# Attention kernel of two layers: statistics of x from four buffers, low weight halves on GpSimd, early first rows, VectorE's row loop unrolled by two

## What is computed

```python
def _gn(v, G=32, eps=1e-5):
    g = v.reshape(B_, H_, W_, G, C_ // G)
    m = jnp.mean(g, axis=(1, 2, 4), keepdims=True)
    s = jnp.var(g, axis=(1, 2, 4), keepdims=True)
    return ((g - m) / jnp.sqrt(s + eps)).reshape(v.shape)

# in_data = _gn(x); q, k, v are projections of it, q scaled by 32 ** -0.5
logits = einsum('abhqc,abhkc->abhqk', q, k) + mask_bias + nonbatched_bias[:, None]
weights = softmax(logits, axis=-1)
wavg = einsum('abhqk,abhkc->abhqc', weights, v)
gate = sigmoid(einsum('abld,ed->able', in_data, Wg) + gating_bias)
x = x + einsum('able,oe->ablo', gate * wavg, Wo) + bo
```

## Time and profile before

| | us |
|---|---|
| median of 3 runs | 3712.91 |
| lowest, highest | 3711.34, 3713.08 |
| the profiled execution: its time | 3713.87 |
| its span (first to last instruction) | 3712.1 |

### The profile page before, as it was taken

The page is one execution under the profiler, slowest core; times in us unless marked ns, Lnnn a source line. Parts: engine busy times, 40 slices in busy tenths (PEclk is TensorE's granted clock), DMA queues, the critical chain, the costliest instruction groups (busy, mean ns, idle before and its releaser), DMA issues.

```text
span 3712.1 us, 122419 instructions
## 1 busy us (share of the span) xinstructions
PE 3487.4 (94%) x36360; PEld 2625.9 (71%) x36360; DVE 3470.5 (93%) x11689; ACT 2890.9 (78%) x5393; POOL 3022.9 (81%) x2056
## 2 busy tenths in 40 slices
PE   0499999999999999999969999999999999999997
PEld 0377777777777777777747777777777777777775
DVE  6599999999999999999959999999999999999997
ACT  0388888888888888888857777778777777777785
POOL 1288888888888888888857888888888888888887
PEclk9999999999999999999989999999999999999999
DMA  8555555555555555555535556566556665566653
GB/s 319 176 117 117 116 115 117 114 119 116 116 115 116 117 117 116 115 118 114 117 112 112 118 117 118 116 121 119 117 117 119 117 121 117 117 118 117 119 119 76
DMA packets 450645, 454.09 MB, mean 122 GB/s; under 512 B 42880, under 2 KB 445440, under 8 KB 445968
## 3 DMA queue, kind: packets, MB, share of 16 engines
q1 hardware_dynamic: 241680, 251.85, 38.3%
q10 hardware_dynamic: 208896, 201.38, 19.6%
HBM read 182.39 MB, written 67.24 MB: 67 GB/s over the span
## 4 chain that ended last, share of the span: by engine, by line
PE 92%; DVE 3%; DMA 3%; issue 1%; POOL 1%; SPq 1%; ACT 1%; DVEq 0%; POOLq 0%; ACTq 0%
PE proj_b L743 19%; PE proj_a L743 18%; PE av_bank L770 13%; PE max_bank L754 13%; PE exp_bank L759 12%; PE proj_a L797 9%; PE den_bank L777 6%; PE proj_b L788 2%; DMA bias_k<-in_xT 1%; DVE stats L589 1%; DMA k_stack<-k_lo 1%; DVE max_bank L656 1%; DVE probs L669 0%; SPq L334 0%; POOL probs_sum L415 0%
## 5 line engine op out<-in xcount | busy, mean ns | idle before, releaser
L656 DVE CUSTOM_DVE_ANT_0 max_bank<-max_bank,bias_q 128x256 f32<-128x256 f32 x4096 | 1643.8, 443 | 156.4 <-PE max_bank L754 132.5
L415 POOL TENSOR_TENSOR probs_sum<-probs 128x1024 f32<-128x1024 f32 x512 | 1208.2, 2360 | 291.2 <-ACT probs L439 152.5
L669 DVE TENSOR_TENSOR probs<-exp_bank,bias_k 128x512 f32<-128x512 f32 x2048 | 1391.7, 680 | 7.4 <-PE exp_bank L759 7.4
L754 PE MATMUL max_bank<-k_stack,q_stack 96*128 96x256 f16 (+1 forms) x4096 | 788.0, 273 | 13.9 <-DMA k_stack<-k_lo 11.9
L759 PE MATMUL exp_bank<-q_stack,k_stack 100*128 100x256 f16 x4096 | 783.2, 272 | 9.6 <-DVE probs L669 6.3
L439 ACT ACTIVATE probs<-probs,mask_bias 128x1024 f32<-128x1024 f32 x512 | 572.8, 1148 | 61.4 <-DVE probs L669 61.2
L656 DVE DVE_READ_ACCUMULATOR2_ANT row_max<- 128x1 f32 x4096 | 573.1, 140 | 0.0
L442 ACT ACTIVATE probs<-probs 128x1024 f32<-128x1024 f32 x512 | 524.7, 1053 | 51.4 <-DVE probs L669 51.4
L770 PE MATMUL av_bank<-probs,v_sb 128*32 128x256 f32 x8192 | 549.3, 386 | 3.1 <-ACT probs L439 1.6
L754 PEld LDWEIGHTS max_bank<-k_stack,q_stack 96*128 96x128 f16 (+1 forms) x4096 | 381.2, 98 | 166.0 <-DVE row_max L656 104.3
L759 PEld LDWEIGHTS exp_bank<-q_stack,k_stack 100*128 100x128 f16 x4096 | 394.2, 97 | 72.6 <-DVE probs L669 11.5
(11 more groups left out here) (132 smaller groups left out, 7049.9 us busy)
## 6 DMA issues: line engine op xcount, KB each, us to landing
q_stack<-q_hi SPq DMA_DIRECT2D x512, 128.0 KB
k_stack<-k_hi SPq DMA_DIRECT2D x512, 128.0 KB
x_in<-in_xT ACTq DMA_DIRECT2D x128, 256.0 KB, 2.7
q_stack<-q_lo SPq DMA_DIRECT2D x256, 128.0 KB
k_stack<-k_lo SPq DMA_DIRECT2D x256, 128.0 KB
y<-in_xT ACTq DMA_DIRECT2D x128, 256.0 KB, 2.9
layer_out<-y ACTq DMA_DIRECT2D x128, 256.0 KB, 2.7
x_in<-layer_out ACTq DMA_DIRECT2D x128, 256.0 KB, 2.7
```

The costliest lines, as they stand in the source:

```text
L415: pool.tensor_tensor(probs_sum[:, g], pr[:, :, 0, :], pr[:, :, 1, :], ALU.add).then_inc(sum_ready, 1)
L656: op = dve.tensor_tensor_reduce(out=max_bank[h % 2][:, t, :], in0=max_bank[h % 2][:, t, :], in1=bias_q[:, h, t, :], scale=1.0 / FINE, scal ...
L669: dve.tensor_tensor(probs[:, r.ring(2), h], exp_bank[h % 2][:, :, :], bias_k[:, h], ALU.add).then_inc(logits_ready, 1)
L754: op = pe.matmul(bank_[:, t, :], q[0:n, t * P:(t + 1) * P], k[0:n, :], start=True, stop=True)
```

## The change

It touches four places. (1) `STAT_TOK` becomes 1024 and there are four buffers of 1 MB, each of the two old ones cut in half: 32 pieces instead of 16. SyncE issues the first four pieces ahead of everything else, then the weights, the mask, the constants, and the rest of the pieces in two loops; the loads of rows 0 and 1 into `x_in` stand between these loops. VectorE's statistics are cut into two loops as well, with the preparation of the mask between them. (2) The low halves of the weights go from VectorE (10 scalar_tensor_tensor) to GpSimd, which needs two instructions for each (a product in place, then a difference). (3) ScalarE loads the table of the square root before it waits for the spread; for layer 1, rows 0 and 1 of x1 are loaded by SyncE in the slot after the last row of layer 0. (4) VectorE's row loop holds two slots instead of four, three kinds of waits are gone or replaced (`shift_psum`, `gate_ready`; `av_psum` and `sum_ready` become `den_psum`), and `gate_tanh` is addressed by a register.

```diff
-STAT_TOK = 2048
+STAT_TOK = 1024
 STAT_LOADS = ROWS * TOK // STAT_TOK
+STAT_BUFS = 4
...
+    def ring_slice(self, n):
+        if isinstance(self.turns, int):
+            return bass.ds(self.off % n, 1)
+        return bass.ds((self.turns * self.unroll + (self.off + n)) % n, 1)
...
-        x_stat = [t.rearrange("p h t k -> p (h t k)").rearrange("p (c t) -> p c t", c=CT)
-                  for t in (probs[:, 1], bias_k[:, :, :, :])]
+        x_stat = [t.rearrange("p h t k -> p (h t k)").rearrange("p (i c t) -> p i c t", i=2, c=CT)[:, i]
+                  for t in (probs[:, 1], bias_k[:, :, :, :]) for i in range(2)]
...
+            def load_stat(c):
+                for i in range(STAT_BUFS):
+                    wait(sp, stat_used, STAT_BUFS * c + (i + 1 - STAT_BUFS), sp_passed)
+                    sp.dma_start(x_stat[i], channel_major(a["xT"], c * (STAT_BUFS * STAT_TOK) + i * STAT_TOK, STAT_TOK)
+                                 ).then_inc(stat_in[i], 16)
...
+                    if l == 0 and s.off == ROWS:
+                        sp.wait_ge(x_norm_ready, ROWS)
+                        for i in range(2):
+                            sp.wait_ge(y_out[i], 16 * (ROWS // 2 - 4))
+                            sp.dma_start(x_in[:, i], channel_major(x1, i * TOK, TOK)).then_inc(x_loaded[i], 16)
...
+            def low_weights(stage, hi, lo):
+                pool.tensor_scalar(stage, stage, W_SCALE, 1.0, ALU.mult, ALU.mult).then_inc(w_scaled, 1)
+                pool.wait_ge(w_scaled, next(scaled))
+                pool.tensor_tensor(lo[:, :, :], stage, hi[:, :, :], ALU.subtract).then_inc(w_lo_ready, 1)
...
                 r = s.plus(2)
-                if r.active():
+                if r.active() and s.active():
...
             for l in range(2):
+                act.preload_act_table_set("sqrt_and_others")
                 act.wait_ge(norm_avg, 2 * l + 2)
...
-                if h == 0:
-                    wait(dve, shift_psum, r.plus(-2).count(1, 1))
                 wait(dve, max_psum, r.count(8, h + 1), dve_passed)
...
-                    wait(dve, av_psum, r.plus(-2).count(2, h // 4 + 1))
-                    wait(dve, sum_ready, r.plus(-2).count(2, h // 4 + 1))
+                    wait(dve, den_psum, r.plus(-2).count(2, h // 4 + 1))
...
                 dve.wait_ge(av_psum, r.count(2, 2))
-                dve.wait_ge(gate_ready, r.count(1, 1))
                 wait(dve, gated_ready, r.plus(-1).count(1, 1))
-                dve.scalar_tensor_tensor(out=avg[:, :, :], in0=gate_tanh[:, r.ring(4)], scalar=1.0,
+                dve.scalar_tensor_tensor(out=avg[:, :, :], in0=gate_tanh[:, r.ring_slice(4)].rearrange(
+                    "p o g t -> p (o g) t"), scalar=1.0,
...
-                slots(dve, l, slot)
+                slots(dve, l, slot, 2)
```

More of the change, by code:

```diff
@@ L30 @@
+import itertools
 import concourse.bass as bass
@@ L271, in _ @@
                 sp.dma_start(out_bias[:, i, :], a[n]).then_inc(const_in, 16)
[L272 to L286, removed]
+            with sp.Fori(1, 3) as c:
+                load_stat(c)
             sp.wait_ge(zeroed, 3)
@@ L289, in _ @@
                 sp.dma_start(stack[1][MASK_ROW:MASK_ROW + 4, i], a["k_rows"]).then_inc(stack_init, 16)
+            for i in range(2):
+                sp.dma_start(x_in[:, i], channel_major(a["xT"], i * TOK, TOK)).then_inc(x_loaded[i], 16)
+            with sp.Fori(3, STAT_LOADS // STAT_BUFS) as c:
+                load_stat(c)
             sp.wait_ge(mask_step, 3)
@@ L358, in _ @@
             pool.wait_ge(zeroed, 3)
+            for l in range(2):
+                for m in range(4):
+                    pool.wait_ge(w_hi_ready, 4 * l + m + 1)
+                    low_weights(w_stage[:, l, m], w_hi[l][m], w_lo[l][m])
+            for l in range(2):
+                pool.wait_ge(w_hi_ready, 8 + l + 1)
+                low_weights(w_out_stage[:, l], w_out_hi[l], w_out_lo[l])
             pool.wait_ge(const_in, 96)
@@ L569, in _, with statistics @@
         def _(dve):
[L571 to L581 removed]
             n = STAT_TOK // 512
[L584 to L585 removed]
+            def statistics(c):
+                for i in range(STAT_BUFS):
                     dve.wait_ge(stat_in[i], c * 16 + 16)
@@ L588, in _ @@
                         for t in range(n):
-                            op = dve.bn_stats(stats[:, ct, bass.ds(c * (2 * n) + (i * n + t), 1), :],
+                            op = dve.bn_stats(stats[:, ct, bass.ds(c * (STAT_BUFS * n) + (i * n + t), 1), :],
                                               x_stat[i][:, ct, t * 512:(t + 1) * 512])
                     op.then_inc(stat_used, 1)
+            with dve.Fori(0, 3) as c:
+                statistics(c)
             dve.wait_ge(mask_in, 32)
@@ L603, in _ @@
             dve.tensor_scalar(mask_pc[:, 1, :], mask_row[:, :], 1.0 / FINE, None, ALU.mult).then_inc(mask_step, 1)
+            with dve.Fori(3, STAT_LOADS // STAT_BUFS) as c:
+                statistics(c)
             def normalisation(l):
```

47 lines of the change are left out of this document (23 added, 24 removed).

## The result

The changed kernel takes a median of 3687.42 us (six executions, 3683.72 to 3689.72) against 3712.83 us for the kernel before (six, 3711.34 to 3713.72). The ratio is 0.9928, with a 95% interval of 0.9917 to 0.9939: faster by 0.7%, 25.4 us. The forecast was 3682.4, in a range of 3673 to 3694.

What follows compares the result with a forecast made beforehand. The prediction took the rows as bound by TensorE, with VectorE close behind, and the start by x's loads and small steps. Savings of 20.8 + 8.1 + 1.6 = 30.5 us gave 3682.4 us, range 3673 to 3694.

Steps and rivals of the forecast that it cites:

- The statistics: Start of the kernel: with four buffers, statistics end at 98 us and aggregation starts 20.8 us sooner, between 17 and 24.
- VectorE can nearly keep up: Statistics: a piece costs VectorE 2.42 us against 2.5 for its data, and the buffers' stock makes up for mask instructions.
- The slow stream: Rival, statistics: a stream that never pauses runs at 361 GB/s, not 421, giving 3693.7 us; chance 0.10.
- The gap that stays: Rival, statistics: halved pieces come in pairs with 2.06 us between, only other savings stay, about 3709 us; chance 0.03.
- Weights on GpSimd: Start: GpSimd does the low halves in about 25 us, done at 50, at the worst 60; cost nothing.
- From the aggregation to the first row: Start of layer 0: x_norm no longer waits for x_in or the square root's table, -8.1 us.
- The change of layers: Between the layers: the square root's table leaves the path and x_in is loaded earlier, -1.6 us.
- The loop: VectorE's row loop: worth 0, with bounds of 0.025 us a row either way over 232 rows, 6 us.
- the shorter cycle: Rival, row loop: VectorE's fewer waits bring fine_shift 0.05 us earlier a row, 11.6 us, giving 3670.8; chance 0.04.
- the dearer turn: Rival, row loop: the loop costs more than its slack; at 0.5 us a row 3724 us; chance 0.03.
- The sum: Whole kernel: 20.8 + 8.1 + 1.6 = 30.5 us saved, the median going from 3712.91 to 3682.4 us.

Runs made afterwards that it cites:

- e7: Changed kernel with rows 0 and 1 of both layers loaded by ScalarE's queue behind the spread, as before: 3688.20 us (one execution).
- e3: Changed kernel with the four small k_rows loads issued behind the last piece of x instead of in the middle of the stream: 3685.71 us, ratio 0.9921.
- e2: Changed kernel with each bn_stats reading 256 of its 512 elements, all loads kept, output differing from the reference: 3686.27 us (one execution).
- e6: Changed kernel with the low halves of the weights back on VectorE, behind the first four pieces: 3688.32 us (one execution).
- e5: Changed kernel with two statistics buffers of 2 MB instead of four of 1 MB: 3698.68 us (one execution).
- e1: Changed kernel with VectorE's old row loop: four slots, the old waits, gate_tanh addressed by a number: 3688.36 us, ratio 0.9928.
- e10: The changed kernel run once more, unedited: 3686.72 us, ratio 0.9925.
- e11: The changed kernel with VectorE's old row loop, the same kernel as e1, run again: 3687.68 us, ratio 0.9926.
- e12: Changed kernel with fine_shift ahead of the logits of head 5, and VectorE's old loop and waits: 3628.78 us, ratio 0.9768.
- e4: Changed kernel with fine_shift ahead of the logits of head 5 in step 1 instead of behind: 3628.51 us, ratio 0.9764.
- e8: Changed kernel with fine_shift ahead of the logits of head 5 and k_rows behind the last piece of x: 3627.16 us, ratio 0.9763.
- e9: Kernel before the change with one edit, fine_shift ahead of the logits of head 5 in step 1: 3657.87 us, ratio 0.9847.

## Why the prediction was right, point by point

- **The statistics** were to end at 98 us and ended at 101.41: 17.4 us won where 20.8 were forecast, inside the 17 to 24 given. The mechanism was right (piece 5 was awaited near 25.5 and began at 25.29), though VectorE began at 6.02 and not near 5, and the first reload was issued at 19.04 and not near 11, neither at a price. Two sizes were off. The rate was taken as 421 GB/s, from a stretch of ten microseconds; over 20 it is 410, which is 2.56 us a piece and not 2.50, so 28 x 0.06 = 1.7 us. And k_rows with `x_in` were priced by their bytes, 0.6 MB, at 2 us. They cost 3.6: `x_in` 1.56, near the 1.28 that its bytes take at 410 GB/s (e7), and k_rows, a ninth of the bytes, another 2.06 (e3). 1.7 + 1.6 are the missing 3.4 us but for 0.1.
- **"VectorE can nearly keep up"** was right: e2 shows the data as the bound, e6 a VectorE that catches up at 4.75 us a pair. The cover of 7.5 us behind a reload held, since no wait of 2 us follows an issue.
- **The slow stream**, the rival of 10%, is settled: 361 GB/s was the mean of a stretch with gaps. That stretch of 20 us held 1.6 cycles; over a whole one, 4.2 MB in 12.38 us, the mean is 339, so 361 was no level of its own. After the change no such gap is there, and the rate from 60 to 80 us is 410. The trace so disagrees with the rule that went with the rival, of about 358 GB/s on the HBM side (the Trainium skill, "DMA: Bandwidth & Descriptors", section "Where 436 GB/s comes from"), with this one core at work. **The gap that stays** would have needed pieces in pairs with a wait; e5 shows what that looks like, and it is not what the change shows.
- **Weights on GpSimd** at no cost was right. The product took 0.62 us where 1.3 was guessed, so the work ended at 39.4 and not at 50. That the step brings nothing either (e6) the prediction didn't ask.
- **From the aggregation to the first row** -8.1 us were forecast. `x_norm` starts 7.39 us behind the aggregation, against 15.47 before (134.31 - 118.84): -8.1. The first maximum was at 123.75 and waited for TensorE alone: `bias_q`, issued at 99.11, had landed 7.9 us later and `bias_k`, issued at 101.41, 10.5 later. The part of `x_in` in this is smaller than the wait of 6.83 us suggested: when it is loaded late it costs 3.89, less the 1.56 that it takes from the stream (e7).
- **The change of layers** was to give 1.6. The square root's table now stands ahead of the wait for `spread`, `x_norm` follows `std` after 1.52 us without a wait, and in e7 1.56 us of wait for `x_in` come back: the mechanism was right. From the start of `spread` to `x_norm` it is 1.77 us (1894.93 to 1896.70) against 3.41 before, 1.64 less. The rows behind it show -1.3 at row 138, and in the same kernel again -0.5, so from the rows the size of this term can't be read to better than a microsecond.
- **The loop** was put at 0, within 0.025 us a row. It is worth 0.003 us a row (e1, e10, e11, e12). Neither of the rivals about it, the shorter cycle or the dearer turn, occurred.
- **The sum** was -30.5 and is -28.4 in the spans. From one to the other: +3.4 at the statistics, -1.6 that no step had foreseen between `x_norm` and row 0 (25.5 us earlier at the one, 27.1 at the other), -0.7 in the rows from 0 to 126, +0.3 at the change of layers, and some +0.6 behind row 138. Against the medians the forecast is 5.0 us too low, and 3 of those come from the two executions that happened to be profiled, one above and one below its median. The 1.6 us were luck: they made up for half of what the statistics fell short, and without them the forecast would have been 6.6 us too low, still inside its range.

The 1.6 us are TensorE's granted clock. Busy time by stretch at the first maxima of row 0, in the kernel before and, 25.5 us earlier, in the changed one:

```profile
148.50:151.80 3.30, 2.95 (x14) 2.11 (x15) 1.64 (x8) 0.00 (x0) 0.00 (x0) 0.51 0.10 29
```

```profile
123.00:126.30 3.30, 3.10 (x29) 2.77 (x30) 2.50 (x12) 1.09 (x2) 0.00 (x0) 1.00 0.03 10
```

In one TensorE runs at 1.2 GHz (granted 0.51) and issues 14 matmuls, in the other at 2.4 (granted 1.00) and issues 29. Both had come from a stretch in which it did little: 1.80 us of 4 busy (144.5 to 148.5) and 1.34 of 4 (119 to 123), each at full clock. The traces of all fourteen runs part in the same way. Where the lower level falls on the first maxima (before, e1, e4, e5, e8, e9), row 0's fine_shift starts 28.2 to 28.6 us behind `x_norm`; in the other eight it is 26.6 to 26.8. As e1 shows the lower level with the changed kernel's start and e11, the same kernel, doesn't, this is a difference between executions. Both traces with the old start show it and four of the twelve with the new one do; whether the new start makes it rarer, and what decides it, stays open.

## What to carry to other kernels

A stage that loads in turn into two buffers loses the time from an issue to its data at each turn, and the mean rate of such a stretch says nothing about what the memory can give: here four buffers of half the size took it from 339 GB/s over a whole cycle to 410, which was half of the gain. Then look at the one instruction that the busiest engine waits for in each turn of the loop, and at what stands ahead of it on its own engine without need: one swap of two VectorE instructions brought 58 us, where the careful rearrangement of the start brought 25. A trace of an engine that is 99.4% busy (1391.81 us of 1400) had hidden that, because overlapping matmuls are counted as busy while the next one waits; what shows it is the distance from the start of one matmul to the next. For the same reason the 1400 of 1400 us in e4 do not prove that nothing is left there.

## What the runs showed of the hardware

- **A load into four partitions holds up a stream.** Four loads of 16 KB, 64 KB together, took the DMA engines from 410 to about 75 GB/s for 2.5 us, although the share of busy DMA time stayed full (1.17 from 42.5 to 45 us); moved away, 2.06 us came back (e3). The Trainium skill, "SBUF — State Buffer", section "Door 1: The DMA port swizzle (why `[64,N]` ≈ `[32,N]`)", says that the rate depends on how many of 16 ports the partitions reach, and by its table the four used here, 96 to 99, lie on one. An estimate from that and the measured rate: a sixteenth of 410 GB/s is 26, at which 64 KB take 2.5 us. The trace agrees with it, though no run here varied the number of partitions, and all four loads also read the same 16 KB, a rival that no run tests.
- **An issue can be slow.** Four loads of weights were issued in 1.97 us before; behind four queued megabytes the same four took 4.16 and then 5.93 us. The first reload was so issued at 19.04 and not near 11. It cost nothing, as the DMA engines were full (share 1.09 from 12 to 25.2 us).
- **VectorE beside a busy stream:** eight `bn_stats` show 5.02 us where they wait for pieces in between and 4.83 where they don't (e6). Waits shorter than some tenths of a microsecond are inside such a group and in no list of waits; half the work per instruction (e2) brings them out, as 1.15 us at each piece, of which 1.06 are the work left out.
